# Divided down products and ScalarE row normalisation in a fused cross-attention and mixture-of-experts kernel

## The reference

```python
h = layernorm(x)
query, key, value = h @ Wq.T, ctx @ Wk.T, ctx @ Wv.T
sim = einsum('bqd,bkd->bqk', query, key)
sim = (sim - mean(sim)) * rsqrt(var(sim) + EPS)      # over each batch's whole matrix
x = x + softmax(sim) @ value @ Wo.T

h = layernorm(x)
swiglu(a | b) = silu(a) * b
shared = swiglu(h @ sw1 + sb1) @ sw2 + sb2
cw = softmax(h @ gate_w + gate_b), all but the two largest of 8 set to 0
routed = sum over e of cw[e] * (swiglu(h @ rw1[e] + rb1[e]) @ rw2[e] + rb2[e])
x = x + shared + routed
```

## Time and profile before

| | |
|---|---|
| median of 3 runs | 141.31 us (140.18 to 141.46) |
| the profiled execution, whole time | 139.67 us |
| its span, first to last instruction | 137.5 us |
| granted TensorE clock, mean | 1.000 |
| TensorE busy | 127.9 us (93%) |
| VectorE busy | 104.0 us (76%) |
| ScalarE busy | 71.4 us (52%) |
| GpSimd busy | 22.8 us (17%) |

### The profile page before, as it was taken

How to read it: one execution, slowest core, us unless ns; L and a number is a source line. 1 busy time by engine, 2 the same in 40 slices (tenths; PEclk the granted TensorE clock), 3 DMA queues, 4 the chain that set the end, 5 groups by cost and what they waited for, 6 DMA issues and landing times.

```text
span 137.5 us, 2015 instructions
## 1 busy us (share of the span) xinstructions
PE 127.9 (93%) x607; PEld 92.7 (67%) x607; DVE 104.0 (76%) x307; ACT 71.4 (52%) x136; POOL 22.8 (17%) x40
## 2 busy tenths in 40 slices
PE   0997997988999999999999999999999999999992
PEld 0775785857777756677776676787567767676772
DVE  1578978677999998929967999629997882956662
ACT  1546869894523239962623269944232975223240
POOL 7083223056250020320400020000400000000000
DMA  4999300000920000059100002088000104900022
GB/s 121 302 349 269 85 0 7 0 2 13 325 124 0 5 0 0 7 170 390 50 5 0 0 0 76 5 262 350 5 0 0 65 16 170 406 36 0 0 81 76
DMA packets 8828, 12.97 MB, mean 94 GB/s; under 512 B 1321, under 2 KB 6994, under 8 KB 8306
## 3 DMA queue, kind: packets, MB, share of 16 engines
q1 hardware_dynamic: 8242, 12.62, 26.6%
q10 hardware_dynamic: 576, 0.23, 0.7%
HBM read 11.73 MB, written 1.11 MB: 93 GB/s over the span
## 4 chain that ended last, share of the span: by engine, by line
PE 48%; issue 31%; POOL 8%; DVE 5%; ACT 3%; DMA 2%; POOLq 0%; DVEq 0%
PE bank L905 42%; POOL row_powers L367 3%; POOL w_rest L391 3%; DMA ctx_sb<-in_ctx_dram 2%; POOL ln_rstd L376 2%; PE bank L967 1%; PE bank L921 1%; POOL sim_r L382 1%; PE bank L995 1%; ACT xn L490 1%; PE bank L1018 1%; DVE x L818 1%; PE bank L1078 1%; DVE g_beats L760 1%; PE bank L913 1%
## 5 line engine op out<-in xcount | busy, mean ns | idle before, releaser
L527 ACT ACTIVATE silu<-bank,b_cols 128x512 f32<-128x512 f32 (+1 forms) x37 | 25.0, 678 | 39.7 <-PE bank L905 39.2
L905 PE MATMUL bank<-x_head,w_head 128*128 128x512 f32 x72 | 38.9, 541 | 0.0
L905 PE MATMUL bank<-act,w_sb 128*128 128x512 f32 x68 | 34.7, 592 | 0.0
L797 DVE TENSOR_TENSOR silu<-silu,cw_all 128x512 f32<-128x512 f32 (+1 forms) x31 | 20.8, 670 | 12.3 <-DMA cw_all<-cw_dram 8.1
L805 DVE SCALAR_TENSOR_TENSOR act<-bank,b_cols,silu 128x512 f32<-128x512 f32 (+1 forms) x37 | 27.2, 737 | 3.3 <-ACT silu L527 1.5
L905 PE MATMUL bank<-x_head,w_rest 128*128 128x512 f32 x72 | 28.5, 395 | 0.0
L905 PE MATMUL bank<-x_rest,w_head 128*128 128x512 f32 x72 | 28.2, 392 | 0.0
L905 PEld LDWEIGHTS bank<-x_head,w_head 128*128 128x128 f32 x72 | 13.6, 189 | 7.5 <-issue 3.1
L905 PEld LDWEIGHTS bank<-x_rest,w_head 128*128 128x128 f32 x72 | 13.7, 190 | 6.3 <-issue 5.0
L905 PEld LDWEIGHTS bank<-x_head,w_rest 128*128 128x128 f32 x72 | 13.5, 188 | 3.2
L905 PEld LDWEIGHTS bank<-act,w_sb 128*128 128x128 f32 x68 | 12.6, 189 | 2.6
(11 more groups left out here) (117 smaller groups left out, 177.3 us busy)
## 6 DMA issues: line engine op xcount, KB each, us to landing
cw_all<-cw_dram SPq DMA_DIRECT2D x4, 1024.0 KB, 6.9
cw_all<-cw_dram SPq DMA_DIRECT2D x4, 512.0 KB, 4.9
cw_all<-cw_dram SPq DMA_DIRECT2D x6, 256.0 KB, 3.6
x_sb<-in_x_dram SPq DMA_DIRECT2D x4, 256.0 KB, 4.8
w_sb<-in_L_ffn_rw_dram SPq DMA_DIRECT2D x1, 1024.0 KB, 7.6
ctx_sb<-in_ctx_dram SPq DMA_DIRECT2D x4, 192.0 KB, 4.8
out_dram<-x SPq DMA_DIRECT2D x3, 256.0 KB, 2.1
w_sb<-in_L_ffn_rw_dram SPq DMA_DIRECT2D x1, 512.0 KB, 7.1
```

The source lines that it names most:

```text
L527: scalar.activation(silu[:, k, cols], hid(n, 0)[:, cols], ACT.Silu, bias=b1_cols[:, 0, e:e + 1]).then_inc(silu_sb, 1)
L797: dve.tensor_tensor(silu[:, k, cols], silu[:, k, cols], cw_all[:, e - 1, cols], ALU.mult).then_inc(scaled_sb, 1)
L905: return pe.matmul(dst, lhs, rhs, start=start, stop=stop, skip_group_check=True)
```

## The change

Twelve of the 34 down products that go through `down` (n = 9, 12, 13, 18, 21, 22 and 27 to 32, the list `DIVIDED`) become three F32R products each. ScalarE writes the head of act(n) in step n + 1, right behind silu(n + 1); VectorE writes its rest in step n + 1, ahead of scale(n + 1) where that expert is 0 or 1, and between scale(n + 1) and act(n + 1) otherwise. The heads of w2 are written by ScalarE at the ends of steps 5 and 6 (5 and 4 experts), the rests in one instruction by VectorE at the end of step 9. And the normalisation of chunks 1 to 3 moves from VectorE to ScalarE: `second_shift` takes the place of `second_normalise` on VectorE, and `normalise` (L490's form) stands on ScalarE in step 3, 12 and 21, behind silu of that step (in step 12 also behind the copies of chunk 3's inputs, u and v).

```diff
+        w2_head, w2_rest = sb("w2_head", [P, NX, D], F32R), sb("w2_rest", [P, NX, D], F32R)
+        act_head, act_rest = sb("act_head", [P, 3, N], F32R), sb("act_rest", [P, 3, N], F32R)
...
-        ACT_AT = {..., 'exponentials': [0, 2], 'prob_copies': [2, 2], ...}
-        DVE_AT = {..., 'residual': [3, 2], 'second_normalise': [4, 2], 'router_logits': [8, 0], ...}
+        ACT_AT = {..., 'exponentials': [0, 2], 'normalise': [5, 1], 'prob_copies': [2, 2], ...}
+        DVE_AT = {..., 'residual': [3, 2], 'second_shift': [4, 2], 'router_logits': [8, 0], ...}
...
+        DIVIDED = [n for n in range(NX, LAST - STRAIGHT) if n >= NX * (C - 1) or n % NX in (0, 3, 4)]
+        W2_GROUPS = [(0, 5), (5, NX)]
+        def divided(n):
+            return DIVIDED.index(n) + 1
...
-            def first_chunk_normalise(g):
-                scalar.wait_ge(shift_sb, g + 1)
-                for i in batch_tiles(groups(0)[g]):
-                    last = scalar.activation(xn[:, i, :], x1[:, i, :], ACT.Identity, bias=ln_shift[:, i:i + 1], scale=ln_rstd[:, i:i + 1])
+            def normalise(c, g):
+                scalar.wait_ge(shift_sb, upto(c, g))
+                if c >= 1:
+                    scalar.wait_ge(x2t_ps, done(c - 1))
+                for i in batch_tiles(groups(c)[g]):
+                    last = scalar.activation(xn[:, i, :], x1[:, TC * c + i, :], ACT.Identity, bias=ln_shift[:, i:i + 1], scale=ln_rstd[:, i:i + 1])
                 last.then_inc(xn_ready, 1)
...
+            def w2_heads(g):
+                lo, hi = W2_GROUPS[g]
+                scalar.wait_ge(w2_in, 32)
+                copy(w2_head[:, lo:hi, :], w2_sb[:, lo:hi, :]).then_inc(w2_head_sb, 1)
+            def act_heads(n):
+                scalar.wait_ge(act_sb, n + 1)
+                copy(act_head[:, n % 3, :], act[:, n % 3, :]).then_inc(act_head_sb, 1)
...
                 if n >= 1:
                     expert_silu(c, e)
+                if n - 1 in DIVIDED:
+                    act_heads(n - 1)
...
+                if n in (5, 6):
+                    w2_heads(n - 5)
...
+            def w2_rests():
+                dve.wait_ge(w2_head_sb, len(W2_GROUPS))
+                dve.tensor_tensor(w2_rest[:, :, :], w2_sb[:, :, :], w2_head[:, :, :].bitcast(F32), ALU.subtract).then_inc(w2_rest_sb, 1)
+            def act_rests(n):
+                dve.wait_ge(act_head_sb, divided(n))
+                dve.tensor_tensor(act_rest[:, n % 3, :], act[:, n % 3, :], act_head[:, n % 3, :].bitcast(F32), ALU.subtract).then_inc(act_rest_sb, 1)
...
-                expert_gate(c, e, lambda: run(n, 1))
+                if n - 1 in DIVIDED and e <= 1:
+                    act_rests(n - 1)
+                def between():
+                    if n - 1 in DIVIDED and e >= 2:
+                        act_rests(n - 1)
+                    run(n, 1)
+                expert_gate(c, e, between)
                 if n == 0:
                     first_statistics(2)
+                if n == NX:
+                    w2_rests()
...
-                pe.wait_ge(act_sb, n + 1)
-                mm(OUT_B[:, :], w2_sb[:, e, :], act[:, k, :], e == 0, n in (NX * (c + 1) - 1, LAST - STRAIGHT)).then_inc(y_ps, 1)
+                first, final = e == 0, n in (NX * (c + 1) - 1, LAST - STRAIGHT)
+                if n in DIVIDED:
+                    pe.wait_ge(w2_rest_sb, 1)
+                    pe.wait_ge(act_rest_sb, divided(n))
+                    mm(OUT_B[:, :], w2_head[:, e, :], act_head[:, k, :], first, False)
+                    mm(OUT_B[:, :], w2_rest[:, e, :], act_head[:, k, :], False, False)
+                    mm(OUT_B[:, :], w2_head[:, e, :], act_rest[:, k, :], False, final).then_inc(y_ps, 1)
+                else:
+                    pe.wait_ge(act_sb, n + 1)
+                    mm(OUT_B[:, :], w2_sb[:, e, :], act[:, k, :], first, final).then_inc(y_ps, 1)
```

More of the change, by code:

```diff
@@ L149, in xattn_moe_kernel @@
         w1_head_sb, w1_rest_sb = [sem(f"w1_head_sb{g}") for g in range(4)], [sem(f"w1_rest_sb{g}") for g in range(4)]
+        w2_head_sb, w2_rest_sb = sem("w2_head_sb"), sem("w2_rest_sb")
         setup_ps, setup_sb = sem("setup_ps"), sem("setup_sb")
@@ L168, in xattn_moe_kernel @@
         act_sb, y_ps = sem("act_sb"), sem("y_ps")
+        act_head_sb, act_rest_sb = sem("act_head_sb"), sem("act_rest_sb")
         out_ps, outt_sb, tok_ps, final_sb = sem("out_ps"), sem("outt_sb"), sem("tok_ps"), sem("final_sb")
@@ L261, in xattn_moe_kernel @@
         PE_AT = {'transpose_inputs': [-4, 1], 'project_u': [-4, 2], 'project_v': [-4, 2], 'scores': [-3, 1], 'scores_average': [-1, 4], 'attend': [3, 4], 'transpose_x2': [6, 4], 'router': [7, 4], 'transpose_cw': [10, 4], 'transpose_prob': [1, 4]}
-        ACT_AT = {'input_copies': [-4, 1], 'u_copies': [-4, 1], 'v_copies': [-4, 1], 'exponentials': [0, 2], 'prob_copies': [2, 2], 'x2_heads': [7, 0], 'router_exp': [9, 1], 'cw_copy': [10, 1]}
-        DVE_AT = {'first_statistics': [-8, 0], 'statistics_0': [-4, 2], 'x2_rests': [7, 0], 'statistics_1': [-2, 0], 'variance': [-1, 1], 'scale': [-1, 2], 'residual': [3, 2], 'second_normalise': [4, 2], 'router_logits': [8, 0], 'router_select': [8, 2], 'router_weights': [9, 0]}
+        ACT_AT = {'input_copies': [-4, 1], 'u_copies': [-4, 1], 'v_copies': [-4, 1], 'exponentials': [0, 2], 'normalise': [5, 1], 'prob_copies': [2, 2], 'x2_heads': [7, 0], 'router_exp': [9, 1], 'cw_copy': [10, 1]}
+        DVE_AT = {'first_statistics': [-8, 0], 'statistics_0': [-4, 2], 'x2_rests': [7, 0], 'statistics_1': [-2, 0], 'variance': [-1, 1], 'scale': [-1, 2], 'residual': [3, 2], 'second_shift': [4, 2], 'router_logits': [8, 0], 'router_select': [8, 2], 'router_weights': [9, 0]}
         POOL_AT = {'first_rstd': [-9, 1], 'scores_rstd': [-2, 0], 'second_rstd': [4, 0]}
@@ L567, in _ @@
             ctx_copy(2)
-            first_chunk_normalise(0)
+            normalise(0, 0)
             v_copy(1)
@@ L573, in _ @@
             copy(b1_cols[:, :, :].rearrange("p h e -> p (h e)"), bank[0][:, 0:2 * NX]).then_inc(setup_sb, 1)
-            first_chunk_normalise(1)
+            normalise(0, 1)
             u_copy(2)
@@ L596, in _ @@
                       "prob_copies": prob_copies, "x2_heads": lambda c: x2_heads(c, 0),
-                      "router_exp": router_exp, "cw_copy": cw_copy}
+                      "normalise": lambda c: normalise(c, 0), "router_exp": router_exp, "cw_copy": cw_copy}
             for n in range(NX * C):
@@ L650, in second_shift @@
                 dve.wait_ge(ln_r[1], upto(c, g))
+                if c >= 1:
+                    dve.wait_ge(xn_ready, done(c - 1))
                 dve.scalar_tensor_tensor(ln_shift[:, t], ln_mv[:, 1, t, 0], -1.0, ln_rstd[:, t], ALU.mult, ALU.mult).then_inc(shift_sb, 1)
[L653 to L660, removed]
             def scores_statistics(m):
@@ L883, in _ @@
                       "variance": scores_variance, "scale": scores_scale, "residual": attention_output,
-                      "second_normalise": lambda c: second_normalise(c, 0), "x2_rests": lambda c: x2_rests(c, 0),
+                      "second_shift": lambda c: second_shift(c, 0), "x2_rests": lambda c: x2_rests(c, 0),
                       "router_logits": router_logits, "router_select": router_select, "router_weights": router_weights}
```

## The result

| | before | after |
|---|---|---|
| median of 22 runs each | 140.34 us (139.69 to 141.46) | 139.47 us (138.56 to 141.02) |
| ratio, 95% interval | | 0.9932 [0.9906, 0.9958] |
| span of the profiled execution | 137.5 us | 136.9 us |

The changed kernel is 0.7% faster (0.4 to 0.9%), inside the bound of 1%: 2 us were taken out of TensorE, and 0.6 (profile) to 0.95 us (ratio) of gain are left. The forecast was 0.4 us faster (140.9 us, where before's median was then 141.31).

The account below looks back on a forecast made before the run. TensorE (93% busy) bounds the last chunk but waits for VectorE's full in-order queue where chunks are prepared. Terms -0.42 - 0.17 + 0.50 + 0.62 - 0.17 - 0.75 = -0.4 us give 140.9 us; own range 140.0 to 141.8, wide 139.0 to 142.5.

Parts of the forecast that it names:

- TensorE's saving: Twelve down products: 0.86 us in float32 becomes three of 0.232 us, 0.17 us each, 2.0 us if all count.
- Chunk 1, 0.4 us, and down(9), 0.17: Chunk 1: `x2_rests` starts with its head, all up to `cw_cols` 0.42 us earlier; down(9) saves 0.17 us more.
- Chunk 2, loss 0.5: Rest of act(13) in VectorE's full stretch makes `cw_cols` and TensorE's transposes 0.50 us later; bounds 0 to 0.6.
- Chunk 3, loss 0.6: Normalisation and the rest of act(21) delay `x2_rests`; router starts at 103.1 and not 102.48; bounds 0.1 to 1.0.
- ScalarE sits waiting: Chunk 3: ScalarE waits for the shift behind rstd, normalises 98.05 to 99.75; silu(22) ends at 100.35, not 98.56.
- silu(22) passed on without harm: Chunk 3: with this and a cheap copy, the loss would be only 0.1 us, its lower bound.
- Normalisation on ScalarE, 1.7 us: Four ScalarE instructions in a row take about 1.7 us by the profile row; the skill's table gave 1.2.
- Last chunk, gain 0.75: down(27) to down(32) save 6 x 0.17 = 1.05 us, less 0.3 lost at down(28).
- The wait at down(28): Last chunk: DMA sets act(28), its rest is ready at 119.45; TensorE starts about 119.6 instead of 119.28, 0.3 lost.
- The loop over three engines: Last chunk: act, head, rest about 2.06 us against TensorE's 2.09; rival: 2.4 us, sum +1.75, 143.1 us, chance 0.15.
- TensorE everywhere: Rival: TensorE sets the end everywhere, all twelve products and chunk 1 count: -2.4, 138.9 us; chance 0.20.
- No gain in chunk 1: Rival: silu and TensorE set the pace in chunk 1, so the sum is 0.0, 141.3 us; chance 0.15.

Follow-up runs that it names:

- e2: Changed kernel with the normalisation of chunks 1 to 3 back on VectorE, only the twelve divided products left: ratio 1.0029 to the kernel before, loop 109.18 us.
- e1: Changed kernel without any divided down product, only the normalisation of chunks 1 to 3 on ScalarE: ratio 0.9958 to the kernel before, loop 108.28 us.
- e8: Normalisation on ScalarE, no divided products, three one-element memsets added on VectorE in step 0: ratio 0.9967 to the kernel before, loop 108.93 us.
- e4: Changed kernel with eight products divided, 12, 13, 18 and 21 left in float32: ratio 0.9913 to the kernel before, loop 107.41 us.
- e3: Changed kernel with the normalisation of chunk 3 alone back on VectorE: ratio 0.9934 to the kernel before, loop 108.24 us.
- e6: Changed kernel with ScalarE copying act(n) twice for n = 28 to 32: ratio 1.0131 to the kernel before, loop 110.21 us.

## Why the prediction was right, and where it was not

The sum (0.4 us gained) was near the 0.6 of the profile and the 0.6 to 1.3 of the ratio's interval, with the mechanism as stated: in the stages of chunk 2 and 3, and at down(28), TensorE waits for VectorE, and what it was spared ends there. The terms were less exact than the sum: the first stage gained 0.33 more than forecast and the third lost 0.12 less, while the last gained 0.21 less, so that errors of two signs partly cancel. The absolute time was not as good: 139.47 us lies below the forecast's own range (140.0 to 141.8) and only inside the wide one (139.0 to 142.5), since the start of 141.31 was the median of 3 runs, and 22 gave 140.34.

- *TensorE's saving*: 0.86 against 3 x 0.232 us, 0.17 each; e2 shows it where TensorE sets the pace (0.13 to 0.21 for one product). Right.
- *Chunk 1, 0.4 us, and down(9), 0.17*: the term was mis-sized. The two gave 0.92 (of which e1 has 0.74 without down(9)). The 0.42 up to the transposes of `cw_cols` came exactly (54.11 to 53.65, less the 0.04 by which the loop began earlier). The rest came behind them: 0.28 of it is VectorE's idle time ahead of scale(7), which went with the place of scale(7) in its queue (e8). I had seen it in no row and had no term for it.
- *Chunk 2, loss 0.5*: 0.48. The rest between scale and act cost 0.5 and not its full 0.69, as worked out, and with it gone (e4) so was the loss.
- *Chunk 3, loss 0.6*: 0.50. The chain of times was right: from the end of rstd to scale(22) 2.58 us forecast and 2.48 measured, to the router 5.28 and 5.18. The reason given in words was not. "ScalarE sits waiting" was seen, but it cost 0.05 (e1, e4). The prediction's own times say so too: before, scale(22) already began at 100.27, and the forecast had it at 100.4. What it did not do is compare the two, that is, take off the 1 us that VectorE no longer spends on the normalisation. The rest of act(21) is nearly all of the loss, and so the lower bound of 0.1 "silu(22) passed on without harm" could not be had with that rest in place.
- *Normalisation on ScalarE, 1.7 us*: 1.65. The Trainium skill's table ("VectorE: DVE Perf Modes", TRN2 errata) would have had 1.2; the measurement decides against it. The Trainium skill's page "ScalarE: Activation LUTs" (What ACT_TABLE_LOAD costs) fits: by its fixed part and its slope, 93 ns for each per-partition operand and 93 ns of overlap, an estimate of 479 ns for one and 1.64 us for four.
- *Last chunk, gain 0.75*: 0.54. The wait at down(28) was there and was mis-sized: 0.43 us (119.57, where six products and the bias end at 119.14) and not 0.3, and the first product after the wait takes 0.31 us to the next one and not 0.23. The 0.12 more of wait is the DMA, which landed 6.05 us behind the transposes and not 5.93 as before: where it landed at 5.93 (e3) the wait was 0.32 us and the gain 0.67. The loop over three engines was 2.04 us (2.06 forecast) and TensorE's step 2.09, so it did not bind; e6 shows that it does when a head is 0.51 us longer. The rival had the right mechanism and not its condition.
- *TensorE everywhere (rival)*: e2 rules it out. *No gain in chunk 1 (rival)*: e1 rules it out, with 0.74 us.

## What to carry to other kernels

Work taken off an engine that is 93% busy is worth something only in the stages where that engine sets the pace; the same work put on an in-order queue that is full in one stage costs its full step there, so choose place by place (nine products beat twelve by 0.8 points of a per cent). Where an operation is moved from one engine to another, net the two: the time that its old engine gets back is what the new wait on the other may use up. A chain that goes act, head, rest, act over two engines can be the bound while each of them shows idle time in every turn. And where a stage starts with a DMA, compare runs in which it landed equally late: here a few tenths of a microsecond came from that alone.

## What the runs showed of the hardware

- A VectorE instruction of 4 elements took 1.60 us in the changed kernel, where GpSimd was subtracting two tensors from SBUF beside it. VectorE's and GpSimd's timelines:

```profile
38.14 1.60 DVE L679 SCALAR_TENSOR_TENSOR ln_shift<-ln_mv,ln_rstd 128x4 f32<-128x4 f32 x1
```

```profile
37.90 1.82 POOL L402 TENSOR_TENSOR w_rest<-w_sb,w_head 128x768 fp32r<-128x768 f32 x1
```

  It ends at 39.74, 0.02 us behind GpSimd's 39.72; the other two shifts took 0.16 us. The Trainium skill ("SBUF — State Buffer", section on the two separate sides) says of a VectorE instruction with two inputs from SBUF and a GpSimd instruction that reads SBUF that the one that starts first holds the shared port for its whole instruction and the other is blocked; this trace agrees. The 2.44 us of `second_normalise` in chunk 1 are 1.3 us more than the 1.12 of chunk 3, and GpSimd's subtraction ran beside it too, so they were probably in good part this wait. The move saved VectorE only about 0.85 us there (scale(3) at 39.66 in place of 40.53, where the forecast had 38.4). It was enough, since the next bound was the head for `x2_rests`, which ended at 44.05.
- VectorE can sit idle for 0.21 to 0.26 us ahead of an instruction that has nothing to wait for, at a place that goes with how many instructions stand ahead of it in its queue (seven cases, at the 192nd and the 320th). It cost 0.28 us in the first stage and about 0.15 in the third. A change of a few tenths of a microsecond in such a kernel can come from that alone.
- The landing of the routing weights varied by up to 0.45 us between profiled executions (scale(28) 5.85 to 6.30 us behind the transposes), and where act(28) sets the pace the stage varied with it.
- The stage ahead of the loop varied by 1.9 us between profiled executions (first hidden product at 25.32 to 27.20 us), three times what the change gained.
